# Graph attention, experts and convolution on one core: softmax moved under the projections, last groups of three tiles, a stage's weights fetched earlier

## What is computed

```python
# 1 attention over the edges that start at a node, 8 heads
q, k, v = (x_norm @ W + b for W, b in ((Wq, bq), (Wk, bk), (Wv, bv)))
ws = einsum('ehd,ehd->eh', q[origin], k[destination]) * SCALE * edge_weights
e = exp(ws - segment_max(ws, origin)[origin])
att = e / (segment_sum(e, origin)[origin] + 1e-16)
values = segment_sum(att[:, :, None] * v[destination], origin)
x = x + (x_ln + (values @ W1 + b1) @ W2 + b2)
# 2 16 experts of 32 hidden units, weights from two softmaxes and two top-2 picks
h = silu(xf @ W1[e]) * (xf @ W3[e]);  out += tw[:, e] * (h @ W2[e])
# 3 twice: diag * (x @ W0) + segment_sum(edge_vals * (x @ W1)[src], dst) + b, relu
# 4 8 experts, top-2: out += w * layernorm(xf + relu(xf @ w1[e] + b1[e]) @ w2[e] + b2[e])
```

## Times and profile before

| | us |
|---|---|
| median of 3 runs (2732.6 to 2736.74) | 2734.81 |
| the profiled execution | 2727.9 |
| its span | 2726.2 |
| mean granted clock | 0.942 |
| sort, 0 to 59 | PE busy 40.76 |
| projections, 59 to 341 | PE busy 228.05, DVE 123.77 |
| softmax, 341 to 401 | PE busy 0.14, DVE 48.82 |
| aggregation, 401 to 493 | PE busy 85.39, DVE 63.15 |
| dense stage's start, 493 to 565 | PE busy 26.16, DVE 43.70 |
| dense stage, 565 to 1389 | PE busy 790.70, DVE 603.34 |
| convolution, 1491 to 2021 | PE busy 523.08 |
| second dense stage, 2130 to 2726 | PE busy 565.80 |

### The profile page before, as it was taken

The page is one execution under the profiler, slowest core; times in us unless marked ns, Lnnn a source line. Parts: engine busy times, 40 slices in busy tenths (PEclk is TensorE's granted clock), DMA queues, the critical chain, the costliest instruction groups (busy, mean ns, idle before and its releaser), DMA issues. The chain is left out here.

```text
span 2726.2 us, 33928 instructions
## 1 busy us (share of the span) xinstructions
PE 2408.2 (88%) x10873; PEld 1874.7 (69%) x10876; DVE 1765.9 (65%) x4090; ACT 1137.3 (42%) x2072; POOL 676.4 (25%) x655
## 2 busy tenths in 40 slices
PE   5698919389999999999948999999989499999998
PEld 4465606277777777777836888888867377777776
DVE  7454277477777777777635675555556377777775
ACT  6453301244544544544324222222224566665651
POOL 5444400211211112111013122221222433333310
PEclk9799958699999999999979999999989699999999
DMA  4112001412212122121053334433336556666631
...
DMA packets 156290, 272.16 MB, mean 100 GB/s; under 512 B 35634, under 2 KB 36274, under 8 KB 155894
## 3 DMA queue, kind: packets, MB, share of 16 engines
...
...
## 5 line engine op out<-in xcount | busy, mean ns | idle before, releaser
L1049 POOL TENSOR_TENSOR d_rs<-d_ve,net_half_neg 128x4 f32<-128x4 f32 x60 | 70.4, 1174 | 529.0 <-DVE d_ve L1105 428.5
L1984 ACT ACTIVATE conv_h<-conv_h 128x512 f32<-128x512 f32 x80 | 50.6, 632 | 311.4 <-DVE conv_h L1936 311.4
L2431 POOL DMA_INDIRECT next_own<-message,d_at x80 | 129.2, 1615 | 168.9 <-DMA next_own<-own 136.7
L1906 DVE TENSOR_TENSOR conv_yl<-conv_pty,conv_yh 128x512 fp32r<-128x512 f32 x80 | 55.3, 691 | 154.2 <-ACT conv_yh L1980 145.0
L65 PE MATMUL conv_p<-conv_w_hi,conv_yh 128*128 128x512 f32 x320 | 134.2, 419 | 0.6 <-DVE conv_yl L1906 0.6
L1062 POOL DMA_INDIRECT d_val<-values,d_at x80 | 86.0, 1076 | 192.2 <-DVE d_x L1187 172.0
L65 PE MATMUL d_po<-d_w_hi,d_hh 128*128 128x512 f32 x320 | 130.3, 407 | 2.5 <-DVE d_x L1200 0.4
L65 PE MATMUL d_pc<-d_xh,d_w_hi 128*128 128x512 f32 x320 | 131.5, 411 | 0.0
L65 PE MATMUL d_pa<-d_xh,d_w_hi 128*128 128x512 f32 x320 | 130.0, 406 | 0.3 <-DVE d_w_lo L1122 0.3
L1378 ACT ACTIVATE d_act_out<-d_pa 128x512 f32<-128x512 f32 x80 | 46.7, 583 | 199.2 <-PE d_pa L67 199.2
L65 PE MATMUL conv_p<-conv_w_hi,conv_hh 128*128 128x512 f32 x320 | 126.1, 394 | 2.0 <-DVE conv_hl L1906 1.9
...
## 6 DMA issues: line engine op xcount, KB each, us to landing
d_x<-in_x SPq DMA_DIRECT2D x20, 1024.0 KB, 7.0
...
```

Source lines behind the costliest of these rows:

```text
L1049: pool.tensor_tensor(rs[n][:], ve[n][:], k.half_neg[:, 0:T], ALU.pow).then_inc(pow_done[n], 1)
L1906: v.tensor_tensor(lo[:, t % 2, :], bank[t % 2][:], hi[:, t % 2, :].bitcast(F32), ALU.subtract)\
L1984: act_.activation(h[:, t, :], h[:, t, :], ACT.Relu).then_inc(h_made, 1)
L2431: pool.indirect_dma_start(own[n][:, t, :], None, k.message2[:, :], bass.IndirectOffsetOnAxis(ap=at[:, t:t + 1], axis=0), bounds_check=EP + ...
```

## The change

**Running softmax.** `Softmax` replaces the scans over 8 x 2560. The eight heads stand four times on the 128 partitions (32 apart), so that one tensor holds high and low parts of two results. For each group of 512 edges one forward scan gives the running maximum (`att_level`); two exponentials come out of one ACT instruction: the factor by which everything so far is rescaled when the maximum rises ("old") and the edge's own term ("new"). A second scan gives the running sum, and after a reciprocal both are divided by it. The aggregation's scan then uses "old" as its factor in place of the flags. The steps for group g-1 run during group g: DVE's `levels` between its splits of the destination rows, ACT's `exponents` after the Q copies, DVE's `parts` at the end of the iteration (in the last group ahead of the destination flags' diagonals), ACT's `high` ahead of the next group's Q copies (in the last after the attribute copy), DVE's `low` after the next first split. For the last group all of it stands after the last V copy. The flags of the sources are spread in group 0 instead of 1, the scores are made on 128 partitions (`headsel4`, `attr4`, filled by `widen`), and K's product is written into `qs`. W1 W2 goes to memory in the sort, ahead of the records' read on SP, and comes back in the last group, where ACT and DVE split it between the V chunks.

**Early fetch.** At the aggregation's start SP loads the first, third and router weights of layer 2 and two groups of rows. ACT makes the high parts in groups 1 to 3, POOL the low parts. They lie where the Q, K, V weights were. In layer 2 only the second weight is loaded and split at the start; the first group is turned in four PSUM banks; its first two chunks of both up products stand ahead of the mix; POOL's constants come after the second gather. The aggregation's loops are written out, and its spreads are two fast matmuls (new, old) in three banks each.

**Last groups of three tiles.** `tiles(g)` and `cols(g)`: the last group of layers 2, 3 and 4 has 3 tiles; in 2 and 4 its wide operations have 288 of 512 columns.

```diff
--- before.py
+++ after.py
+NROWS = -(-N // P) * P
+LAST = -(-(N - (NG - 1) * GR) // P)
+LAST_COLS = (N - (NG - 1) * GR) // 32 * 32 + 32
+def tiles(g):
+    return LAST if g == NG - 1 else T
+def cols(g):
+    return slice(0, LAST_COLS if g == NG - 1 else GR)
...
+class Softmax:
+    def levels(self, v, g, same, part):
+        s, m = self.steps, self.level
+        if part == 0:
+            if g:
+                s(v.tensor_copy(m[:, 0:1], m[:, GR:GR + 1]))
+                s(v.tensor_copy(self.total[:, 0:1], self.total[:, GR:GR + 1]))
+            else:
+                s(v.memset(m[:, 0:1], 0.0))
+                s(v.memset(self.total[:, 0:1], 0.0))
+            s.link(v.tensor_scalar(self.pen[:], same[:, g * GR:g * GR + GR], -1.0, 1e30, ALU.add, ALU.mult))
+            s.link(v.tensor_tensor_scan(m[:, 1:GR + 1], self.pen[:], self.score[:], m[:, 0:1], ALU.add, ALU.max))
+        elif part == 1:
+            s.link(v.tensor_tensor(self.expo[:, 0, :], m[:, 0:GR], self.pen[:], ALU.add))
+            s(v.tensor_tensor(self.expo[:, 0, :], self.expo[:, 0, :], m[:, 1:GR + 1], ALU.subtract))
+        else:
+            s(v.tensor_tensor(self.expo[:, 1, :], self.score[:], m[:, 1:GR + 1], ALU.subtract))
+    def exponents(self, act_, g):
+        act_.activation(self.expo[:], self.expo[:], ACT.Exp).then_inc(self.exp_done, 1)
+    def parts(self, v, g):
+        s, low, up = self.steps, slice(0, P // 2), slice(P // 2, P)
+        old, new, scale = self.expo[:, 0, :], self.expo[:, 1, :], self.level[:, 0:GR]
+        v.wait_ge(self.exp_done, g + 1)
+        s.link(v.tensor_tensor_scan(self.total[:, 1:GR + 1], old, new, self.total[:, 0:1], ALU.mult, ALU.add))
+        s.link(v.tensor_scalar(scale, self.total[:, 1:GR + 1], 1e-16, None, ALU.add))
+        s.link(v.reciprocal(scale, scale))
+        s(v.tensor_tensor(new[low], new[low], scale[low], ALU.mult))
+        s.link(v.tensor_tensor(new[up], old[up], self.total[up, 0:GR], ALU.mult))
+        s(v.tensor_tensor(new[up], new[up], scale[up], ALU.mult))
+    def high(self, act_, g):
+        act_.activation(self.mixed[:, g * GR:g * GR + GR], self.expo[:, 1, :], ACT.Copy).then_inc(self.high_made, 1)
+    def low(self, v, g):
+        v.wait_ge(self.high_made, g + 1)
+        for q in (1, 3):
+            rows, at = slice(q * QUAD, q * QUAD + QUAD), slice(g * GR, g * GR + GR)
+            self.steps(v.tensor_tensor(self.mixed[rows, at], self.expo[rows, 1, :], self.mixed[rows, at].bitcast(F32),
+                                       ALU.subtract))
...
+            sp.wait_ge(hi_made, 4 * KC)
+            sp.dma_start(chunks(k.w12), w12[:]).then_inc(r.w12_out, 16)
             sp.wait_ge(stored, 16 * 4)
             sp.wait_ge(scattered, ET * 16)
             sp.dma_start(k.rec["s"][:], k.rec_s[0:EP, :].rearrange("(t p) w -> p t w", p=P)).then_inc(sorted_in, 16)
...
-    flagged = {1: "s", EG - 1: "d"}
+    flagged = {0: "s", EG - 1: "d"}
...
+        sp.wait_ge(r.w12_out, 16)
+        sp.wait_ge(turned["s"], 4 + 4 * EG)
+        sp.dma_start(w12[:], chunks(k.w12)).then_inc(w12_in, 16)
...
+        def widen(g):
+            v.wait_ge(attr_turned, g + 1)
+            v.tensor_copy(attr4[:].rearrange("p t (r n) -> p t r n", n=QUAD)[:, :, :, 0:HEADS],
+                          rec["s"][:, T * g:T * g + T, 2:2 + HEADS].bitcast(F32).unsqueeze(2).broadcast_to([P, T, 4, HEADS]))\
+             .then_inc(attr_wide, 1)
...
             last = g == EG - 1
             for t in range(T):
                 split_lo(v, g, "d", t, t % 2)
+                if g >= 2 and t == 0:
+                    soft.low(v, g - 2)
+                if g and t:
+                    soft.levels(v, g - 1, same["s"], t - 1)
             if not last:
                 s = statistics(v, g + 1, "s")
             else:
                 place("d")
+                soft.parts(v, g - 1)
             if g in flagged:
                 diagonal(flagged[g], 0)
                 diagonal(flagged[g], 1)
...
                 v.wait_ge(k_done, 4 * g + cc + 1)
                 v.wait_ge(q_out, 4 * g + cc + 1)
-                v.wait_ge(score_done, 4 * g + cc + 1)
-                v.scalar_tensor_tensor(prod[:, cc % 2, :], pp[cc % 2][:], bias[:, 1, cc:cc + 1], qs[:, cc, :],
+                v.scalar_tensor_tensor(qs[:, cc, :], pp[cc % 2][:], bias[:, 1, cc:cc + 1], qs[:, cc, :],
                                        ALU.add, ALU.mult).then_inc(k_out, 1)
                 if g in flagged and cc < EG - 2:
                     diagonal(flagged[g], cc + 2)
+                if last and cc == 3:
+                    soft.low(v, g - 1)
                 if not last and cc == 1:
                     statistics2(v, g + 1, "s", s)
                 if not last and cc == 2:
...
             compare(g, 0)
             v.wait_ge(attr_out, g + 1)
             v.wait_ge(score_done, 4 * g + 4 + 2)
-            v.tensor_tensor(scores[:, g * GR:g * GR + GR], p_score[0:HEADS, :], scores[:, g * GR:g * GR + GR], ALU.mult)\
-             .then_inc(score_out, 1)
+            v.tensor_tensor(soft.score[:], p_score[:], soft.score[:], ALU.mult).then_inc(score_out, 1)
             if not last:
+                widen(g + 1)
                 s = statistics(v, g + 1, "d")
                 for t in range(T):
                     split_lo(v, g + 1, "s", t, t % 2)
...
                     number_ranks(range(0, 10))
                 if g == 2:
                     number_ranks(range(10, ET))
+                if g:
+                    soft.parts(v, g - 1)
         v.wait_ge(score_out, EG + 1)
+        for part in range(3):
+            soft.levels(v, EG - 1, same["s"], part)
+        for cc in range(KC):
+            v.wait_ge(w12_high, cc + 1)
+            v.tensor_tensor(lo["wq"][:, cc, :], w12[:, cc, :], hi["wq"][:, cc, :].bitcast(F32), ALU.subtract)\
+             .then_inc(w12_low, 1)
+        soft.parts(v, EG - 1)
+        soft.low(v, EG - 1)
+        v.wait_ge(w12_low, KC)
...
                 split_hi(act_, g, "d", cc, cc % 2)
+            if g:
+                soft.exponents(act_, g - 1)
             act_.wait_ge(attr_turned, g + 2)
             act_.wait_ge(score_out, g + 1)
-            act_.activation(scores[:, g * GR:g * GR + GR], p_attr[0:HEADS, :], ACT.Copy).then_inc(attr_out, 1)
+            act_.activation(soft.score[:], p_attr[:], ACT.Copy).then_inc(attr_out, 1)
+            if last:
+                soft.high(act_, g - 1)
             for i in range(KC):
                 if g in flagged:
                     copy_flags(flagged[g], i)
...
                 if not last and cc >= 2:
                     norm(act_, g + 1, "d", 2 * cc - 4)
                     norm(act_, g + 1, "d", 2 * cc - 3)
+                if last:
+                    act_.wait_ge(w12_in, 16)
+                    act_.activation(hi["wq"][:, cc, :], w12[:, cc, :], ACT.Copy).then_inc(w12_high, 1)
+            if g and not last:
+                soft.high(act_, g - 1)
+        soft.exponents(act_, EG - 1)
+        soft.high(act_, EG - 1)
...
+            cols_ = value[:, cc, g * GR + 1:g * GR + GR + 1]
+            v.tensor_tensor(cols_, cols_, new[n % 3][:], ALU.mult).then_inc(weighted, 1)
+            v.wait_ge(weighted, n + 1)
+            v.tensor_tensor_scan(cols_, old[n % 3][:], cols_, value[:, cc, g * GR:g * GR + 1],
                                  ALU.mult, ALU.add).then_inc(summed, 1)
...
+            for n, source, high, _, _ in coming[g - 1:g] if g else ():
+                act_.wait_ge(early.weight_in[n], 16)
+                for part in range(KC):
+                    act_.activation(high[:, part, :], source[:, part, :], ACT.Copy).then_inc(early.weight_high[n], 1)
+    @block.gpsimd
+    def _(pool):
+        for n, source, high, low_, _ in coming:
+            for part in range(KC):
+                pool.wait_ge(early.weight_high[n], part + 1)
+                pool.tensor_tensor(low_[:, part, :], source[:, part, :], high[:, part, :].bitcast(F32), ALU.subtract)\
+                    .then_inc(early.weight_low[n], 1)
+        for n, _, _, _, _ in coming:
+            pool.wait_ge(early.weight_low[n], KC)
...
+        def spread_weights(g, cc):
+            n, at = 4 * g + cc, slice(g * GR, g * GR + GR)
+            if n >= 3:
+                pe.wait_ge(summed, n - 2)
+            pe.matmul(new[n % 3][:], spreads[0][:, cc * P:cc * P + P], soft.mixed[:, at], start=True, stop=True)
+            pe.matmul(old[n % 3][:], spreads[1][:, cc * P:cc * P + P], soft.mixed[:, at], start=True,
+                      stop=True).then_inc(spread, 1)
...
+        for n, source, _, _, name in coming:
+            sp.dma_start(source, chunks(a[name])).then_inc(early.weight_in[n], 16)
+        for g in range(2):
+            sp.dma_start(early.x[g][:], a["x"][g * GR:(g + 1) * GR, :].rearrange("(t p) n -> p t n", p=P))\
+              .then_inc(early.x_in[g], 16)
...
-            load(0, 0)
-            for n in (0, 3, 1):
-                load_weight(n)
-            load(1, 1)
```

(20 more changed lines are left out.)

564 lines of the change are left out of this document (293 added, 271 removed).

## The result

The changed kernel took 2663.98 us (median of 4 runs, 2660.17 to 2667.44) against 2735.77 for the kernel before (4 runs): a ratio of 0.9739, interval 0.9721 to 0.9756, so 71.8 us faster. The forecast was 2661, range 2635 to 2697. The median agrees better with the forecast than the terms do, and that is in part luck: terms 2 and 3 came out 13.2 higher than said, terms 1, 4 and 5 to 7 together 7.8 lower, and the median lies 3.8 above the profiled execution where 6.9 had been added.

A forecast was written before the change was run, and what follows sets the result against it. PE was taken to bound the busy stretches, and the chain PE waits for the low ones. The terms sum to -73.5 against the profiled 2727.9 us: 2654.4; with the median 6.9 higher, forecast 2661, range 2635 to 2697.

The forecast's parts named there:

- Term 1: Softmax's tail, last V matmul to first weighting: only the last group's chain and part of the border stay; -43.2 us.
- Term 2: Sort and projections: softmax work spread over the edge groups, 12.8 us of DVE each, partly delays PE; +21.2 us.
- the same without row numbers: Projections, group 3: delay like group 2's, mostly covered; with group 4's Q copies +3.3 us.
- Term 3: Aggregation: spreads as two fast matmuls shorten the start and each group's period; -7 us.
- DVE with 13.4 is the bound: Aggregation: PE's work falls from 15.8 to 12.9 us a group, so DVE's 13.4 sets the period.
- Term 4: Dense stage's start: loads, POOL's constants and weight splits leave the chain, routing runs beneath 48 up matmuls; -17 us.
- Terms 5 to 7: Short last groups: first dense stage -13.5, convolution -6.5, second dense stage -7.5; together -27.5 us.
- A: Projections: softmax paid in full on PE's path, 55 in place of 21, time 2695 us; chance 0.15.
- B: Projections: softmax hidden but for last group's K and first loads, 10 in place of 21; 2644 us; chance 0.13.
- D: Last groups: 288 columns cost nearly what 512 do because 188 ns weight loads pace; 2675 us; chance 0.12.
- C: Projections: PE's stalls drop the clock to 1.2 GHz, 166 us more, time 2827 us; chance 0.03.
- one of the signs that I named for a wrong forecast: Projections: granted clock in 60 to 345 us lower than in the kernel before; no size given.

The follow-up runs named there:

- e1: Changed kernel with the last groups full again (four tiles, 512 columns); 2684.11 us, ratio 0.9835 to the kernel before.
- e2: Changed kernel keeping three tiles in the last groups but giving their wide operations 512 columns; 2667.93 us.
- e8: Changed kernel with three of the next group's spreads put ahead of the first output tile in the aggregation; 2659.31 us (one run).
- e10: Changed kernel with 12 up matmuls ahead of the mix instead of 48; first down matmul 68.4 us after SP's first issue, against 68.6; total time not given.
- e4: Changed kernel with `parts`, levels and exponentials on 8 of 512 columns in the first four edge groups (results left out); 2634.44 us (one run).
- e3: Changed kernel with DVE's `parts` on 8 of 512 columns in the first four edge groups, waits kept; 2635.06 us (one run).

## Why the prediction was right, and where its steps failed

- **Term 1** (-43.2, measured -47.8). The chain of the last group was right, 11.6 for 11.1, and so is its premise: the scan lasts 1.28 on 128 partitions, the reciprocal 3.35 against 3.23. The mis-sized step is the border: 6.6 was assumed to stay and 1.5 is left. The tail takes 14.3 in all runs that leave it alone. Before, POOL's scatters of the slots ran up to the border, and SP read them at 343.18; now they end at 358.5 and the read is issued at 359.69, all under V. How much of the rest of the old 8.6 was a wait for that read, and how much the engines' meeting, no run separated.
- **Term 2** (+21.2, measured +18.4 in e1 and e2, +26.2 in the profiled execution). Right in kind: DVE's parts delay ACT's high copies, these the Q copies, and these PE. Right in size too for the pieces that are `parts`: 5.1 at the end of group 2 (5.3 predicted), then 0.4 in group 3 and 9.5 in group 4 (3.3 predicted for group 3 and group 4's Q copies, 8.1 for its K), in all 15.0 for 16.7. But group 3 is not "the same without row numbers": the second half of the ranks stands ahead of the `parts` on which its Q copies wait, and PE's wait there is as long as group 2's, 7.3. It is cheap because waits of 7.0 go for it. The sort, the flags and the wider loads were put at 4.5 and cost 3.4; the sort's 2 did not come (the first Q copy of group 0 is 0.4 later). The profiled execution is 5.0 over the term because of PE's late signals, 7.8, for which I had no term.
- **Term 3** (-7, measured +1.2) failed. The step "DVE with 13.4 is the bound" took the larger of the two engines' sums for the period. Inside a group they do overlap, with PE at 3.26 a tile, and the first output came 5.1 sooner after the first spread, as said. But between groups PE waits for `agg_al`, which waits for the last output; before, eight slow spreads stood in a row in that gap (3.70 us at 427.94), and once they are fast part of the gap is idle. From the last output of a group to the first of the next it was 8.3, 6.7, 8.3 and 5.4 us and is 5.8, 6.9, 6.9 and 6.8, only 2.2 less in all. The spreads now stand between the tiles instead, whose outputs came each 2.63 to 2.81 and come each 3.26. So the 20 outputs take 5.0 longer, 74.0 for 69.0. e8 gets 4.5 of this and pays 2 of it back ahead of the first. The 0.9 a group in the term's sum doesn't follow from its own two figures either (15.8 - 13.4 = 2.4). And the Trainium skill's rule (GPSIMD Engine Reference, 1. Specifications) was laid on the wrong instructions: DVE's products have one operand in PSUM and keep 0.68; only `agg_al` has two in SBUF.
- **Term 4** (-17, measured -17.5). First transpose 17.9 after SP's first issue (16 predicted), third up 52.2 (54.2). The working counted the 48 up matmuls as cover for the routing, and e10 shows that this cover is worth nothing.
- **Terms 5 to 7** (-27.5, measured -31.9 in e1). The columns were right in the first stage, 10.2 for 9.6, and too small in the second, 6.9 for 5.4; the tile was put too small: 6.4 in place of 4.2 in the first stage (2.8 + 1.4 + 1 - 1) and 2.6 in place of 1.9 in the second.
- **Rivals.** A, B and D fall by e1 to e4. C's mechanism is there at small size, and one of the signs that I named for a wrong forecast came true, though the forecast held: the granted clock from 60 to 345 us is 0.87 and was 0.91. Busy time of each engine, clock, DMA share and rate over the projections; the changed kernel, then e3, in which `parts` is short:

```profile
59.00:367.00 308.00, 230.48 (x972) 173.88 (x972) 180.52 (x407) 123.29 (x189) 122.75 (x120) 0.88 0.16 39
```

```profile
59.00:345.00 286.00, 226.13 (x972) 169.89 (x972) 158.05 (x407) 124.15 (x190) 123.21 (x119) 0.91 0.17 42
```

Before it was 0.91 too, over PE's 228.05 busy; e2, without late signals, has 0.87. PE is busy 4.4 us longer than in e3 with as many matmuls: more of them fall to the lower level after the new waits. Between e2 and e3 it is 2.4, 0.2 and 1.8 in groups 2, 3 and 4. That was too little to decide, 4.4 us where C needed 73.5.
